# Ten loads for the next phase: one request of 5 MB, or ten pieces of 512 KB behind the tiles' stores

## Chip, cores and metric

The kernel runs on one core of a Trainium2 chip. A core has five engines with a program each: TensorE (PE: matmuls), VectorE (DVE), ScalarE (ACT), GpSimd (POOL) and SyncE (SP), which here only asks for DMA transfers. The transfers of all engines are carried out by 16 DMA engines. The metric is the time of one execution on the device in microseconds (us), lower is better.

## What is computed

A network of two layers on 4 x 512 tokens of 512 features, each with a mixer and a feed-forward part, a residual and a layer norm behind each. Only the start of the first mixer, a Mamba2 block, matters here:

```python
xz = x @ in_proj_w.T                       # 512 -> 2 x 1024 features
x_branch, z_branch = jnp.split(xz, 2, axis=-1)
y = conv(x_branch, conv_w)                 # causal, 4 taps, per feature
x_branch = silu(y + conv_b)
proj = x_branch @ x_proj_w.T               # 1024 -> X (1024), dt (16), B (128), C (128)
# ... chunked scan with X, dt, B, C ...
Y = Y * silu(z_branch)
return Y @ out_proj_w.T
```

The product `x_proj_w` and all that follows are the next phase. Every product is taken in three matmuls of rounded high and low parts (`product`, L82): hi*hi, hi*lo, lo*hi.

## The kernel before

**The input projection** (`mixer`, L129) handles the tokens in four batches of 512 (`NB` = 4, `SEQ` = 512), and in each batch eight tiles of 128 features (`IT` = 8): 32 tiles, numbered n = 8 b + j from 0 to 31. For each tile PE makes two products, one for the x branch and one for the z branch, of 12 matmuls each (`batch` of PE, L828), into four PSUM banks `acc` in turn: the x product of tile n uses the bank of tile n - 2, and so does the z product. Behind PE the tile passes through this chain (`batch` of ACT, L628, and of DVE, L1065): ACT scales the product with the last tap (L633), DVE adds three taps (L1071), ACT takes the silu (L639) and writes the rounded high part `out_hi` (L642), ACT writes the silu of z, `out_z` (L645), DVE writes the low part `out_lo` (L1062). `out_hi`, `out_lo` and `out_z` have two buffers each, used by even and odd tiles.

**The stores.** SP sends each tile's three results to DRAM, 256 KB each, in the order of its program: `xh` (L349), `zs` (L351), and `xl` of the tile before (L344). ACT may write `out_hi` of tile n only when the store `xh` of tile n - 2 has landed:

```python
act.wait_ge(s_sh[j % 2], turn)                       # L640
```

and PE may start the z product of tile n only when ACT has read z of tile n - 2:

```python
pe.wait_ge(s_zo, n - 1 + 2)                          # L835, s_zo starts at 2
```

Its x product waits in the same way for the taps of tile n - 2 (L837). So a late store holds ACT, and through ACT's queue PE.

**The loads for the next phase.** When the first batch is stored, the buffer `pre` that held the tokens is free, and SP asks for what the next phase reads first: five small tensors (L366 to L369), six of the eight row blocks of `x_wx` (3 MB, L371; `STAGED` = 6), `x_wbc` (1 MB, L372), and the first 128 tokens of `xh` and `xl`, read back from DRAM (512 KB each, L377 and L378, behind a wait for the first batch's stores). All count on one semaphore, `s_early`. Its first readers are in the last batch: ACT at tile 24 (`ahead`, L563) and PE after the first product of tile 24 (L797).

The batches 1 and 2 are a hardware loop on SP, ACT, PE and DVE. Everything is ordered by hand, engine by engine. Nothing plans or reorders.

Of the kernel before, what the change touches and what calls it, by code (L numbers as in the profile page):

```python
# [12 lines left out]
P = 128  # L13
# [5 lines left out]
DI = 2 * DM  # L19
# [109 lines left out]
def mixer(nc, t, ident):  # L129
# [3 lines left out]
    with ExitStack() as ctx:  # L133
# [175 lines left out]
        @block.sync  # L309
        def _(sp):  # L310
            def x_load(c, slot):
                for i, n in enumerate(("xh", "xl")):
                    sp.dma_start(raw(xin[slot][:, i]),
                                 t[n][:, :, bass.ds(c * P, P)].rearrange("j p n -> p j n")).then_inc(s_lx[slot], 16)

            def z_load(c):
                sp.dma_start(z_raw[:], t["zs"][:, :, bass.ds(c * P, P)].rearrange("j p n -> p j n")).then_inc(s_lz, 16)

            def load_x(b):
                sp.dma_start(x_tok[:, b], t["x"][b].rearrange("(c p) d -> p c d", p=P)).then_inc(s_x[b], 16)  # L320

            def load_w(g):
                if g >= 2:
                    sp.wait_ge(s_wlo, g - 1)
                sp.dma_start(w_raw[:, g % 2], t["in_w"][:, g]).then_inc(s_w[g % 2], 16)

            for c in range(CPB):
                sp.dma_start(x_tok[:, 0, c], t["x"][0, c * P:(c + 1) * P, :]).then_inc(s_x0[c], 16)
            load_w(0)
            sp.dma_start(cw[:], t["conv_w"]).then_inc(s_small, 16)  # L330
            sp.dma_start(cb[:], t["conv_b"]).then_inc(s_small, 16)
            load_w(1)
            for b in range(1, NB):
                load_x(b)
                if b + 1 < GRP:
                    load_w(b + 1)
            for i in range(2):
                sp.sem_inc(s_sh[i], 16)
                sp.sem_inc(s_sl[i], 16)
                sp.sem_inc(s_sz[i], 16)  # L340

            def store_lo(b, j):
                sp.wait_ge(s_xl, b * IT + j + 1 + 2)
                sp.dma_start(t["xl"][j][:, bass.ts(b, SEQ)], raw(out_lo[:, j % 2])).then_inc(s_sl[j % 2], 16)  # L344

            def batch(b, last=False):
                for j in range(IT):
                    sp.wait_ge(s_xo, b * IT + j + 1 + 2)
                    sp.dma_start(t["xh"][j][:, bass.ts(b, SEQ)], raw(out_hi[:, j % 2])).then_inc(s_sh[j % 2], 16)  # L349
                    sp.wait_ge(s_zo, b * IT + j + 1 + 2)  # L350
                    sp.dma_start(t["zs"][j][:, bass.ts(b, SEQ)], out_z[:, j % 2]).then_inc(s_sz[j % 2], 16)  # L351
                    if j:
                        store_lo(b, j - 1)
                    if last and j == 3:
                        sp.wait_ge(s_zacc, LASTB * IT + TPG // 2)
                        sp.dma_start(stage(6), t["x_wx"][:, 6]).then_inc(s_wl[0], 16)
                    if last and j == 5:
                        sp.wait_ge(s_zacc, LASTB * IT + TPG)
                        sp.dma_start(stage(7), t["x_wx"][:, 7]).then_inc(s_wl[1], 16)
                        for i in range(2):  # L360
                            sp.wait_ge(s_sz[i], 16 * (IT // 2 + 1))
                        z_load(0)
                store_lo(b, IT - 1)

            batch(0)
            sp.dma_start(wdt[0:NH, 0:DI], t["x_wdt"]).then_inc(s_early, 16)  # L366
            sp.dma_start(wdt[0:NH, DI:DI + NH], t["dtw"]).then_inc(s_early, 16)
            for n, name in enumerate(("dtb", "a_log", "d_skip")):
                sp.dma_start(per_head[:, n], t[name]).then_inc(s_early, 16)  # L369
            sp.wait_ge(s_xT, NB * KT)  # L370
            sp.dma_start(pre[:, 0:STAGED * DI], t["x_wx"][:, 0:STAGED].rearrange("p k n -> p (k n)")).then_inc(s_early, 16)  # L371
            sp.dma_start(pre[:, STAGED * DI:STAGED * DI + IT * 2 * NS],  # L372
                         t["x_wbc"].rearrange("p k n -> p (k n)")).then_inc(s_early, 16)
            for i in range(2):
                sp.wait_ge(s_sh[i], 16 * (IT // 2 + 1))
                sp.wait_ge(s_sl[i], 16 * (IT // 2 + 1))
            sp.dma_start(raw(x0[:, 0]), t["xh"][:, :, 0:P].rearrange("j p n -> p j n")).then_inc(s_early, 16)  # L377
            sp.dma_start(raw(x0[:, 1]), t["xl"][:, :, 0:P].rearrange("j p n -> p j n")).then_inc(s_early, 16)  # L378
            with sp.Fori(1, LASTB) as b:
                batch(b)  # L380
            batch(LASTB, True)
            sp.wait_ge(s_zacc, ROWS)
            x_load(1, 1)
            for i in range(WO):
                sp.dma_start(wo_part(wo_raw, i), t["out_w"][:, i]).then_inc(s_ol[i], 16)
            for i in range(2):
                sp.wait_ge(s_sh[i], 16 * (ROWS // 2 + 1))
                sp.wait_ge(s_sl[i], 16 * (ROWS // 2 + 1))
                sp.wait_ge(s_sz[i], 16 * (ROWS // 2 + 1))

            def step(g, slot, turn, first, left):
                if left == 2:
                    sp.wait_ge(s_p0, g + 1)
                    sp.wait_ge(s_p1, g + 1)
                    x_load(g + 2, 1 - slot)
                if not first:
                    sp.wait_ge(s_x1, g)
                    sp.dma_start(t["x1"][bass.ds(g * P - P, P), :], rr[:]).then_inc(s_out, 16)
                    sp.wait_ge(s_out, 16 * g)
                sp.dma_start(rr[:], t["x_rows"][bass.ds(g * P, P), :]).then_inc(s_lr, 16)  # L400
                if left:
                    sp.wait_ge(s_g, g + 1)
                    z_load(g + 1)
            chunks(sp, step)
            sp.wait_ge(s_x1, NCH)
            sp.dma_start(t["x1"][TOK - P:TOK, :], rr[:]).then_inc(s_out, 16)
            sp.wait_ge(s_out, 16 * NCH)
# [79 lines left out]
        def _(act):  # L487
# [72 lines left out]
            def ahead(j):  # L560

                if j == 0:
                    act.wait_ge(s_early, 144)  # L563
                    act.wait_ge(s_wlo, GRP)
                    nc.scalar.activation(wb_hi[:, :, NH:BC], stage_bc, ACT.Copy).then_inc(s_bwhi, 1)
                if j == 1:
                    act.wait_ge(s_zacc, LASTB * IT)
                    x_weights(0)
                if j == 2:
                    act.wait_ge(s_wdt, 1)  # L570
                    nc.scalar.activation(wb_hi[:, :, 0:NH], WDT.rearrange("p (k n) -> p k n", k=IT),
                                         ACT.Copy).then_inc(s_bwhi, 1)
                    x_weights(1)
                if j == 3:
                    x_weights(2)
                if j == 4:
                    bc_copy(0)
                    b_high(0, True)
                    x_weights(3)
                if j == 5:  # L580
                    nc.scalar.activation(a_pos, a_pos, ACT.Exp).then_inc(s_apos, 1)
                    dt_exp(0)
                    turned_copy(0)
                    c_high(0)
                if j == 6:
                    x_weights(4)
                    act.wait_ge(s_zacc, LASTB * IT + TPG // 2)
                    x_weights(5)
                if j == 7:
                    act.wait_ge(s_sum, 1)  # L590
                    nc.scalar.activation(c_hi[:], CT, ACT.Copy).then_inc(s_ch, 1)
                    x_weights(6)
# [84 lines left out]
        def _(pe):  # L677
# [116 lines left out]
            def ahead(m):  # L794

                if m == 0:
                    pe.wait_ge(s_early, 144)  # L797
                    for kt in range(IT):
                        ins = pe.matmul(WDT[:, kt * NH:(kt + 1) * NH], wdt[0:NH, bass.ts(kt, P)], dtw,
                                        start=True, stop=True)  # L800
                    ins.then_inc(s_wdt, 1)
                if m == 7:
                    pe.wait_ge(s_bwlo, 2)
                    bc_proj(0)
                if m == 9:
                    turn_bc(0, True)
                if m == 11:
                    cb_product(0, True)
                if m == 14:
                    pe.wait_ge(s_tri, 2)  # L810
                    pe.wait_ge(s_const, 6)
                    a_sums(0, True)
# [2056 lines left out]
```

## Time and profile before

| | |
|---|---|
| median of 3 runs | 2368.57 us (2367.68 to 2369.22) |
| profiled execution | 2367.82 us, of which the profile's span is 2366.1 us |
| PE busy | 2271.9 us, 96% of the span |
| DVE, ACT, POOL busy | 1577.5, 888.7, 762.1 us |
| mean granted TensorE clock | 0.987 of full speed (2.4 GHz) |
| DMA | 155.41 MB, mean 66 GB/s |

The times are device times. The profile is of one execution with its own time, 0.75 us under the median. PE is busy nearly throughout, so the time follows PE: what counts is where PE stands idle or runs at the lower clock, and what held it there. In the windows view each line is a stretch of the span and its length, then the busy time and the count of instructions of PE, of PE's weight loads (PEld), of DVE, ACT and POOL, the granted clock, the mean busy share of the DMA engines (it can read slightly over 1 in short stretches) and GB/s. In the timeline each line is an instruction with its start, its duration and, in brackets, the idle time of its engine before it and who ended it. SPq rows are SP's DMA requests: the duration there is the time of the request, not of the transfer. The start-to-start distance of the matmuls is what they cost. Their durations overlap.

### The profile page before, as it was taken

What the parts mean: (1) busy time and instruction counts of PE and PEld (TensorE: products, weight loads), DVE (VectorE), ACT (ScalarE), POOL (GpSimd) and SP (SyncE); (2) the same over time, 40 slices, a digit from 0 to 9 for tenths busy, and PEclk for the clock granted to TensorE, in tenths of its full rate; (3) what the DMA queues carried; (4) which work ended last, traced back from release to release, by engine and by line L of the source; (5) the groups of instructions that cost most, each with busy time, mean ns of one, the idle gap of its engine ahead of it and who ended that gap; (6) DMA issues with size and microseconds to landing.
All of it is one profiled execution on the core that took longest, in us unless ns stands there. A gap on an engine that the chain in (4) does not pass through costs nothing.

```text
span 2366.1 us, 30896 instructions
## 1 busy us (share of the span) xinstructions
PE 2271.9 (96%) x10746; PEld 1864.7 (79%) x10746; DVE 1577.5 (67%) x2392; ACT 888.7 (38%) x1441; POOL 762.1 (32%) x571
## 2 busy tenths in 40 slices
PE   8899999999969999999999899999999899999997
PEld 7787788888857888888887688777778778888885
DVE  5557777777747856674455666576677887766665
ACT  5456333333324322332232444234344434444441
POOL 0002544444412222251111533234233533333331
PEclk9999999999979999999999999999999999999999
DMA  5746222222132001000000111221111021111110
GB/s 205 224 146 188 63 71 71 71 75 74 56 111 107 36 1 36 23 1 19 1 1 27 57 52 55 106 81 54 54 54 54 27 89 54 53 53 53 53 36 36
DMA packets 91015, 155.41 MB, mean 66 GB/s; under 512 B 6288, under 2 KB 55440, under 8 KB 84256
## 3 DMA queue, kind: packets, MB, share of 16 engines
q1 hardware_dynamic: 90912, 154.07, 19.3%
q8 instruction: 61, 1.00, 0.2%
q14 instruction: 42, 0.34, 0.0%
HBM read 114.20 MB, written 39.85 MB: 65 GB/s over the span
## 4 chain that ended last, share of the span: by engine, by line
PE 61%; DVE 6%; issue 2%; ACT 1%; POOL 1%; DMA 0%; SPq 0%; POOLq 0%; DVEq 0%; ACTq 0%
PE attn_pvk L1120 4%; PE attn_pvk L1121 4%; PE attn_pvk L1122 4%; PE attn_pq L1120 2%; PE attn_pq L1121 2%; PE attn_pq L1122 2%; PE attn_po L1120 2%; PE attn_po L1121 2%; PE attn_po L1122 2%; PE attn_pv L1120 2%; PE attn_pv L1121 2%; PE attn_pv L1122 2%; PE attn_pv L85 2%; PE attn_pv L87 2%; PE attn_pv L86 2%
## 5 line engine op out<-in xcount | busy, mean ns | idle before, releaser
L2491 DVE TENSOR_TENSOR moe_a_lo<-moe_up_raw,moe_a_hi 128x512 fp32r<-128x512 f32 x192 | 183.0, 969 | 154.8 <-ACT moe_a_hi L1954 154.7
L1836 POOL TENSOR_TENSOR moe_h_lo<-moe_c_t,moe_h_hi 128x512 fp32r<-128x512 f32 x96 | 128.4, 1337 | 356.3 <-ACT moe_h_hi L1954 356.2
L1120 PE MATMUL attn_pvk<-moe_b_hi,moe_a_hi 128*128 128x512 f32 x512 | 200.9, 392 | 14.0 <-ACT moe_c_last L2080 6.0
L1122 PE MATMUL attn_pvk<-moe_b_hi,moe_a_lo 128*128 128x512 f32 x512 | 199.8, 390 | 0.0
L1121 PE MATMUL attn_pvk<-moe_b_lo,moe_a_hi 128*128 128x512 f32 x512 | 199.8, 390 | 0.0
L1954 ACT ACTIVATE moe_c_t<-attn_pvk 128x512 f32<-128x512 f32 x192 | 113.2, 596 | 186.5 <-PE attn_pvk L1122 184.5
L1231 POOL TENSOR_TENSOR ffn_h_lo<-ffn_h_f,ffn_h_hi 128x512 fp32r<-128x512 f32 x64 | 89.8, 1402 | 266.6 <-ACT ffn_h_hi L1284 266.6
L2006 ACT ACTIVATE moe_c_t<-moe_c_t 128x512 f32<-128x512 f32 x96 | 60.4, 629 | 241.1 <-DVE moe_c_t L2563 241.1
L1427 DVE SCALAR_TENSOR_TENSOR acc<-attn_pvk,ffn_wts,acc 128x512 f32<-128x512 f32 x128 | 91.2, 749 | 88.8 <-PE attn_pvk L87 88.5
L1954 ACT ACTIVATE moe_a_hi<-moe_up_raw 128x512 fp32r<-128x512 f32 x192 | 116.0, 624 | 56.4 <-POOL moe_up_raw L1806 56.4
L1120 PEld LDWEIGHTS attn_pvk<-moe_b_hi,moe_a_hi 128*128 128x128 f32 x512 | 96.4, 188 | 38.0 <-issue 11.3
L2523 DVE SCALAR_TENSOR_TENSOR acc<-attn_pv,moe_wts,acc 128x512 f32<-128x512 f32 x123 | 91.8, 747 | 41.4 <-PE attn_pv L1122 40.4
L1071 DVE SCALAR_TENSOR_TENSOR mix_conv<-mix_acc,mix_cw,mix_conv 128x511 f32<-128x511 f32 (+2 forms) x96 | 71.9, 748 | 69.3 <-ACT mix_conv L633 67.0
L2563 DVE TENSOR_TENSOR moe_c_t<-moe_c_t,attn_po 128x512 f32<-128x512 f32 x128 | 86.4, 684 | 43.2 <-ACT moe_c_t L1954 37.9
L2523 DVE SCALAR_TENSOR_TENSOR acc<-attn_pq,moe_wts,acc 128x512 f32<-128x512 f32 x133 | 99.2, 746 | 22.3 <-PE attn_pq L1122 19.3
L85 PE MATMUL mix_acc<-mix_x_hi,mix_w_hi 128*128 128x512 f32 (+1 forms) x256 | 102.2, 399 | 11.6 <-issue 5.7
L1806 POOL TENSOR_TENSOR moe_up_raw<-moe_up_raw 128x512 f32<-128x512 f32 x32 | 52.0, 1624 | 188.9 <-DVE moe_a_lo L2491 188.8
L1122 PEld LDWEIGHTS attn_pvk<-moe_b_hi,moe_a_lo 128*128 128x128 f32 x512 | 96.4, 188 | 20.3
L1121 PEld LDWEIGHTS attn_pvk<-moe_b_lo,moe_a_hi 128*128 128x128 f32 x512 | 96.4, 188 | 19.5
L1120 PE MATMUL attn_pq<-moe_dn_hi,moe_h_hi 128*128 128x512 f32 x266 | 106.1, 399 | 2.7 <-DVE acc L2523 2.7
L85 PE MATMUL mix_tp<-mix_wx_hi,mix_x 128*128 128x512 f32 x256 | 106.4, 416 | 0.0
L1121 PE MATMUL attn_pq<-moe_dn_lo,moe_h_hi 128*128 128x512 f32 x266 | 104.2, 392 | 0.0
(487 smaller groups left out, 6573.2 us busy)
## 6 DMA issues: line engine op xcount, KB each, us to landing
moe_up_raw<-in_e_up SPq DMA_DIRECT2D x28, 1024.0 KB, 5.7
moe_dn_raw<-in_e_dn SPq DMA_DIRECT2D x28, 512.0 KB, 3.6
xh<-mix_out_hi SPq DMA_DIRECT2D x32, 256.0 KB, 2.6
zs<-mix_out_z SPq DMA_DIRECT2D x32, 256.0 KB, 3.2
xl<-mix_out_lo SPq DMA_DIRECT2D x32, 256.0 KB, 3.4
mix_x<-xh SPq DMA_DIRECT2D x16, 512.0 KB, 4.1
mix_x<-xl SPq DMA_DIRECT2D x16, 512.0 KB, 5.3
mix_z_raw<-zs SPq DMA_DIRECT2D x16, 512.0 KB, 3.9
```

The lines of the kernel that those rows point to most:

```text
L85: pe.matmul(out, lh, rh, start=first, stop=False)
L1071: nc.vector.scalar_tensor_tensor(out=conv[:, j % 2, d:SEQ], in0=acc[:, 2 * j % 4, 0:SEQ - d], scalar=cw[:, j, TAPS - 1 - d:TAPS - d], in1= ...
L1120: pe.matmul(out, lh, rh, start=first, stop=False, skip_group_check=True)
L1121: pe.matmul(out, lh, rl, start=False, stop=False, skip_group_check=True)
L1122: return pe.matmul(out, ll, rh, start=False, stop=True, skip_group_check=True)
L1231: nc.gpsimd.tensor_tensor(h_lo[:, f], h_f[:, f % 2], raw(h_hi[:, f]), ALU.subtract).then_inc(s_hlo, 1)
L1427: stt(out=acc[:, ch], in0=pd[c], scalar=wts[:, ch, bass.ds(F * u + f, 1)], in1=acc[:, ch], op0=ALU.mult, op1=ALU.add).then_inc(s_acc, 1)
L1836: tt(h_lo[:, m, tok], src, raw(h_hi[:, m, tok]), ALU.subtract).then_inc(s_hlo, 1)
L1954: copy = lambda out, src: nc.scalar.activation(out, src, ACT.Copy)
L2491: tt_(a_lo[q][:], src, raw(a_hi[q][:]), ALU.subtract).then_inc(s_alo, 1)
L2523: stt(out=acc[:, ch], in0=bank, scalar=wts[:, ch, w] if isinstance(w, slice) else wts[:, ch, bass.ds(w, 1)], in1=acc[:, ch], op0=ALU.mult, ...
L2563: tt_(c_t[tile][:, i], c_t[tile][:, i], bank(i), ALU.add).then_inc(sem, 1)
```

## The change

SP no longer asks for the 5 MB in one go before batch 1. A new function `ahead(i)` holds ten requests of 512 KB: six row blocks of `x_wx`, two halves of `x_wbc`, and the two read-backs of `xh` and `xl`. One of them stands behind the stores of each tile of batch 1 (i = 0 to 7) and of the first two tiles of batch 2 (i = 8, 9). The wait for the first batch's stores moves to i = 8. The five small loads stay where they were. SP's hardware loop over batches 1 and 2 becomes a Python loop, so its rows are written out. The two waits on `s_early` ask for 15 transfers (16 * 15 = 240) instead of 9 (144).

```diff
+            def ahead(i):
+                if i < STAGED:
+                    sp.dma_start(stage(i), t["x_wx"][:, i]).then_inc(s_early, 16)
+                elif i < STAGED + 2:
+                    k0 = (i - STAGED) * IT // 2
+                    sp.dma_start(stage_bc[:, k0:k0 + IT // 2], t["x_wbc"][:, k0:k0 + IT // 2]).then_inc(s_early, 16)
+                elif i < STAGED + 4:
+                    if i == STAGED + 2:
+                        for n in range(2):
+                            sp.wait_ge(s_sh[n], 16 * (IT // 2 + 1))
+                            sp.wait_ge(s_sl[n], 16 * (IT // 2 + 1))
+                    part = i - STAGED - 2
+                    sp.dma_start(raw(x0[:, part]),
+                                 t[("xh", "xl")[part]][:, :, 0:P].rearrange("j p n -> p j n")).then_inc(s_early, 16)
...
                     if j:
                         store_lo(b, j - 1)
+                    if 0 < b < LASTB:
+                        ahead((b - 1) * IT + j)
...
             sp.wait_ge(s_xT, NB * KT)
-            sp.dma_start(pre[:, 0:STAGED * DI], t["x_wx"][:, 0:STAGED].rearrange("p k n -> p (k n)")).then_inc(s_early, 16)
-            sp.dma_start(pre[:, STAGED * DI:STAGED * DI + IT * 2 * NS],
-                         t["x_wbc"].rearrange("p k n -> p (k n)")).then_inc(s_early, 16)
-            for i in range(2):
-                sp.wait_ge(s_sh[i], 16 * (IT // 2 + 1))
-                sp.wait_ge(s_sl[i], 16 * (IT // 2 + 1))
-            sp.dma_start(raw(x0[:, 0]), t["xh"][:, :, 0:P].rearrange("j p n -> p j n")).then_inc(s_early, 16)
-            sp.dma_start(raw(x0[:, 1]), t["xl"][:, :, 0:P].rearrange("j p n -> p j n")).then_inc(s_early, 16)
-            with sp.Fori(1, LASTB) as b:
+            for b in range(1, LASTB):
                 batch(b)
...
-                    act.wait_ge(s_early, 144)
+                    act.wait_ge(s_early, 16 * (5 + STAGED + 4))
...
-                    pe.wait_ge(s_early, 144)
+                    pe.wait_ge(s_early, 16 * (5 + STAGED + 4))
```

On SP, at the step from batch 0 to batch 1, this stands before, from the last small load on (the `DMA pre` rows are the weights, the `mix_x` rows the read-backs, the rows behind the branch the first tile of batch 1):

```order
L369 DMA mix_heads<-in_d_skip 128x16
L371 DMA pre<-in_x_wx 128x6144 [waits mix_x_transposed]
L372 DMA pre<-in_x_wbc 128x2048
L377 DMA mix_x_50<-xh 128x8x128 [waits mix_x_hi_stored1,mix_x_lo_stored1,mix_x_lo_stored0,mix_x_hi_stored0]
L378 DMA mix_x_50<-xl 128x8x128
L379 UNCONDITIONAL_BRANCH
L379 ISA
L349 ISA [waits mix_x_hi_out]
L349 DMA xh<-mix_out_hi 128x512
L351 DMA zs<-mix_out_z 128x512 [waits mix_z_tile_out]
```

And now, at the same place (L364, L366 and L344 are the stores of xh, zs and xl, L348 is the first branch of `ahead`):

```order
L386 DMA mix_heads<-in_d_skip 128x16
L364 DMA xh<-mix_out_hi 128x512 [waits mix_x_hi_out,mix_x_transposed]
L366 DMA zs<-mix_out_z 128x512 [waits mix_z_tile_out]
L348 DMA pre<-in_x_wx 128x1024
L364 DMA xh<-mix_out_hi 128x512 [waits mix_x_hi_out]
L366 DMA zs<-mix_out_z 128x512 [waits mix_z_tile_out]
L344 DMA xl<-mix_out_lo 128x512 [waits mix_x_lo_out]
L348 DMA pre<-in_x_wx 128x1024
```

Four requests of 5 MB together stood ahead of the first store of batch 1, and none does now. Each tile's stores have one 128x1024 request behind them.

At the end of batch 1 and the start of batch 2, on SP too, this stands now (L351 is the second half of `x_wbc`, L358 the read-backs). The lone L344 row closes batch 1:

```order
L351 DMA pre<-in_x_wbc 128x1024
L344 DMA xl<-mix_out_lo 128x512 [waits mix_x_lo_out]
L364 DMA xh<-mix_out_hi 128x512 [waits mix_x_hi_out]
L366 DMA zs<-mix_out_z 128x512 [waits mix_z_tile_out]
L358 DMA mix_x_50<-xh 128x8x128 [waits mix_x_hi_stored1,mix_x_lo_stored1,mix_x_lo_stored0,mix_x_hi_stored0]
L364 DMA xh<-mix_out_hi 128x512 [waits mix_x_hi_out]
L366 DMA zs<-mix_out_z 128x512 [waits mix_z_tile_out]
L344 DMA xl<-mix_out_lo 128x512 [waits mix_x_lo_out]
L358 DMA mix_x_50<-xl 128x8x128
```

The read-backs moved from ahead of batch 1 to tiles 16 and 17. The instructions of PE, DVE, ACT and POOL, their order and the semaphores they wait on are the same in both kernels.

## Rows read from the trace of the kernel before

**Rows 1.** PE's waits in 60 to 216 us: total, times, longest.

```profile
PE mix_acc L85 <- ACT mix_out_z L645: 5.2, 1, 5.2
PE mix_tp L710 <- DVE mix_cb_m L930: 2.0, 1, 2.0
```

**Rows 2.** Windows: stretch, us, PE, PEld, DVE, ACT, POOL, clock, DMA, GB/s.

```profile
76.00:100.00 24.00, 18.77 (x76) 15.05 (x75) 8.53 (x12) 8.05 (x14) 0.00 (x0) 0.86 0.90 308
92.00:94.00 2.00, 0.00 (x0) 0.00 (x0) 0.00 (x0) 0.47 (x1) 0.00 (x0) 0.50 1.07 305
100.00:162.00 62.00, 62.00 (x275) 51.12 (x273) 34.23 (x48) 29.37 (x48) 1.53 (x8) 1.00 0.51 153
```

**Rows 3.** Timeline of ACT around the stall and where it catches up with PE.

```profile
80.33 0.63 ACT L642 ACTIVATE mix_out_hi<-mix_conv 128x512 fp32r<-128x512 f32 x1
84.60 0.63 ACT L639 ACTIVATE mix_conv<-mix_conv 128x512 f32<-128x512 f32 x1 [2.48 <-DVE mix_conv L1071]
93.53 0.63 ACT L642 ACTIVATE mix_out_hi<-mix_conv 128x512 fp32r<-128x512 f32 x1 [8.30 <-DMA xh<-mix_out_hi]
...
98.66 0.63 ACT L642 ACTIVATE mix_out_hi<-mix_conv 128x512 fp32r<-128x512 f32 x1
103.65 0.63 ACT L642 ACTIVATE mix_out_hi<-mix_conv 128x512 fp32r<-128x512 f32 x1
104.19 0.58 ACT L645 ACTIVATE mix_out_z<-mix_acc 128x512 f32<-128x512 f32 x1
...
134.99 0.78 ACT L633 ACTIVATE mix_conv<-mix_acc,mix_cb,mix_cw 128x512 f32<-128x512 f32 x1 [0.27 <-PE mix_acc L87]
```

**Rows 4.** Timeline of SP's requests around the stall.

```profile
75.05 0.43 SPq L369 DMA_DIRECT2D mix_heads<-in_d_skip  x1
...
77.02 6.44 SPq L378 DMA_DIRECT2D mix_x<-xl  x1
83.82 5.22 SPq L349 DMA_DIRECT2D xh<-mix_out_hi  x1
```

**Rows 5.** Timeline of PE before and behind the stall.

```profile
75.85 0.39 PE L85 MATMUL mix_acc<-mix_x_hi,mix_w_hi 128*128 x1
...
89.22 0.39 PE L87 MATMUL mix_acc<-mix_x_hi,mix_w_lo 128*128 x1
94.84 0.80 PE L85 MATMUL mix_acc<-mix_x_hi,mix_w_hi 128*128 x1 [5.23 <-ACT mix_out_z L645]
...
98.69 0.40 PE L85 MATMUL mix_acc<-mix_x_hi,mix_w_hi 128*128 x1
```

**Rows 6.** DMA requests by line: number, size, median us to landing.

```profile
xh<-mix_out_hi SPq DMA_DIRECT2D x32, 256.0 KB, 2.6
mix_x<-xl SPq DMA_DIRECT2D x16, 512.0 KB, 5.3
pre<-in_x_wx SPq DMA_DIRECT2D x1, 3072.0 KB, 11.4
mix_wx_raw<-in_x_wx SPq DMA_DIRECT2D x2, 512.0 KB, 4.7
```

**Rows 7.** SP's first and last request of tile 27, a 512 KB load.

```profile
185.16 0.33 SPq L349 DMA_DIRECT2D xh<-mix_out_hi  x1
...
186.96 0.46 SPq L356 DMA_DIRECT2D mix_wx_raw<-in_x_wx  x1
```

**Rows 8.** Windows of 1 us in and behind tile 27, and at 203 us.

```profile
188.00:189.00 1.00, 1.00 (x6) 0.84 (x5) 0.00 (x0) 0.00 (x0) 0.00 (x0) 1.00 1.18 207
191.00:192.00 1.00, 1.00 (x7) 0.83 (x6) 0.96 (x2) 0.45 (x1) 0.04 (x1) 1.00 0.00 0
203.00:204.00 1.00, 1.00 (x6) 0.83 (x5) 0.96 (x3) 0.55 (x1) 0.00 (x0) 1.00 1.13 129
```

**Rows 9.** The first reader of the early loads, on ACT.

```profile
162.87 1.90 ACT L565 ACTIVATE mix_wb_hi<-pre 128x2048 fp32r<-128x2048 f32 x1
```

**Rows 10.** A window of 4 us in the next part, with PE busy throughout.

```profile
716.00:720.00 4.00, 4.00 (x12) 3.15 (x11) 2.13 (x5) 1.69 (x2) 0.00 (x0) 0.57 0.96 360
```

## Prediction

> **What bounds the kernel now.** The page says 96% PE, so I read only what keeps PE from working in the stretch that the change touches, 60 to 216 us. PE's waits come first [rows 1]: two of note, 5.2 us for `out_z` of ACT and 2.0 us for a DVE mask near the end of the phase. The windows [rows 2] place the first: between 76 and 100 us PE is busy for 18.77 of 24 us at a mean clock of 0.86, while the DMA engines are busy to 0.90 at 308 GB/s. From 100 to 162 us PE has no gap at all, at full clock, with the DMA engines half idle (0.51). The timeline of ACT gives the cause [rows 3]: `out_hi` of tile 10 is ready to be written at 84.60 + 0.63 = 85.2, but starts at 93.53, 8.30 us late, when the store `xh` of tile 8 has landed. SP's rows say why that store was late [rows 4]. SP was free for it at 75.5, when the last small load (75.05 + 0.43) was asked for. It then asked for the four large loads, the last request took 6.44 us (the queue was full), and the store was asked for at 83.82, took 5.22 us to ask for, and queued behind the 5 MB. The 3 MB load alone takes 11.4 us to land, against 2.6 us for such a store in the median [rows 6].
>
> So this is one stall with one cause: three results of a tile cannot leave because 5 MB that nobody reads until 162.87 [rows 9] stands ahead of them.
>
> **The change part by part.** *The stall.* PE's matmuls follow each other every (89.22 - 75.85) / 59 = 0.2266 us ahead of the stall (59 steps between those two rows of the pattern), so the next one was due at 89.22 + 0.23 = 89.45, and it starts at 94.84 [rows 5]: 5.39 us. *The clock.* Behind the gap the granted clock is 0.50, which is 1.2 GHz [rows 2]. The nine steps from 94.84 to 98.69 take 3.85 us instead of 9 x 0.2266 = 2.04 [rows 5]: 1.81 us. Together 7.20 us of PE's time are lost here.
>
> *What is late next when it goes.* PE, at 89.45, needs ACT to have finished z of tile 10. ACT and DVE go round a tile in 103.65 - 98.66 = 4.99 us when nothing holds them, PE in 24 x 0.2266 = 5.44 us. Without the stall `out_hi` of tile 10 starts at 80.33 + 4.99 = 85.3 and z of it ends about 1.1 us later (z starts 0.54 after `out_hi` and takes 0.58 [rows 3]), at 86.4: 3.0 us ahead of PE. The distance grows by 0.45 us per tile until ACT waits for PE, as it does in the trace from 134.99 on. So nothing on ACT or DVE takes the stall's place, and at tile 24, where the last batch begins, all engines stand to each other as they do now. What follows (the 2.0 us for the mask, the wait at the start of the next part) hangs on PE, ACT and on SP's requests made after them, and moves with them. I give it zero.
>
> *The added requests.* SP gets one more request per tile on ten tiles. Such a request is 0.46 us, behind 1.8 us for the three stores (185.16 to 186.96) [rows 7]. That is 2.3 us of a tile's 5, so it is hidden. A tile now moves 3 x 256 + 512 KB = 1.31 MB. At the 308 GB/s of the crowded stretch that is 4.3 us of a tile's 4.99 to 5.44, so the DMA engines keep up. The trace also has one tile that already looks like the new ones, tile 27, with `x_wx` block 6 behind its stores: from its first request at 185.16 [rows 7] to a silent queue by 191 at the latest [rows 8], under 5.84 us, the requests' 1.8 us included. If I take all of that as transport, every tile hands 0.4 us to the next, 4 us over ten tiles. The room is larger: a store `xh` is asked for some 0.8 us after `out_hi` starts (its 0.63 us and a little), its buffer is wanted 2 x 4.99 us after that start, and it lands in 2.6 us, which leaves 9.98 - 0.8 - 2.6 = 6.6 us. So the added wait is bounded by 0 on both readings. I take 0, and keep the slow readings for the rivals. A gain from smaller stores' queues, below nothing, has no place: PE has no other gap to give back in 100 to 162 us.
>
> *The late loads.* The last piece, the read-back of `xl`, goes out with the stores of tile 17, seven tiles of 5.44 us ahead of those of tile 24, so at about 121 us, and lands in 5.3 us [rows 6]. Its readers come at 162.87 - 7.2 = 155.7: about 29 us of cover. The moved wait, for the stores of batch 0, was passed by 77.02 before [rows 4] and now stands some 38 us later, so it is met. The written-out loop costs SP nothing that PE sees.
>
> The trace bears on a rule here. The 512 KB pieces land in 4.7 us in the median and the 3 MB in 11.4 [rows 6], so six pieces one after another would take 28 us. The Trainium skill ("DMA: Bandwidth & Descriptors", section Bandwidth and its Rules for kernel authors) says to batch transfers to at least 1 MiB, and its fit of a fixed 2.0 us plus bytes over 436 GB/s makes a tile's four transfers an estimated 11.0 us if they went one by one. By the rule the change would hurt: 11.0 us per tile against 5.44 is far past the room above. The trace disagrees for this queue: tile 27's four transfers were over in 5.84 us, so their fixed parts overlap.
>
> *Sum.* -5.39 - 1.81 + 0 = -7.20 us. The profiled execution goes from 2367.82 (span 2366.1 and 1.7 around it) to 2360.6. It is 0.75 under the median of the runs shown, so the median goes from 2368.57 to 2361.4.
>
> **The rivals.** Let t be the time in which the DMA engines move a tile's 1.31 MB. The lag over ten tiles is 10 (t - 5.44), and what exceeds the room of 6.6 us becomes a wait of ACT and of PE.
>
> *Part of the stall comes back.* The slowest 1 us of tile 27 moved 207 GB/s [rows 8]. If all ten tiles went at that, t = 6.33, the lag 8.9 and the wait 2.3 us. With that alone 2363.7, and with a lower clock behind it (1.8 us) 2365.5. I put this case at 2364.6. Against it: 207 was one microsecond with the requests just changing from stores to a load, and the mean of the crowded stretch is 308.
>
> *The pieces choke the stores, slower than before.* From t = 6.82 us on (192 GB/s) the wait exceeds the 7.20 us won. At 168 GB/s, the mean of the two slowest microseconds here (207 and 129 [rows 8], the second with a read-back in 512-byte rows like i = 8 and 9), t = 7.8, the wait 17.0 and the time 2368.6 + 9.8 = 2378.4. For it: in the new kernel eight tiles in a row have a load, not one. Against it: all the rows of longer stretches. The skill's rule above, if it held, would be this case too.
>
> *It does not do what it says.* The first store of batch 1 might be late for another reason than the 5 MB, for instance the small loads ahead of it, or the stall might move to another buffer (`out_lo` or `out_z`, with the same two turns). Then nothing changes: 2368.6. Against it: SP is free at 75.5, before the store's data, and the other stores queue in the same place.
>
> **How the numbers follow.** The forecast case has a chance of 0.86, the partial one 0.07, no change 0.04, slower 0.03. A median of three tells 0.2% (4.7 us) from no change, so faster means under 2363.8. The forecast case's own spread is the clock's: the granted clock also falls in stretches where PE is busy (0.57 in 4 us [rows 10], worth 4 x 0.43 = 1.7 us), and the shift may win or lose one such dip, so 2359.7 to 2363.1. The partial case reaches to 2365.5. I take 2359.6 to 2364.5, which leaves out most of the last two cases, part of the partial one and the tails. Faster: 0.86. The partial and the empty case give 0.11 for no change, and slower has 0.03.
>
> **What would show it.** Right: no PE gap over 1 us between 65 and 160 us, clock 1.00 throughout there. The `xh` store of tile 8 asked for near 76.0 and landed before 85.3. No wait of ACT L651 (now the write of `out_hi`) for a DMA. ACT waits for PE from about tile 13 on instead of 19. ACT's copy of `x_wbc` at about 155.7. The wait for the mask still 2.0 us. DMA share in the tiles of batch 1 near 0.8. Wrong: a DMA wait on `out_hi` or `out_lo` in later tiles with landings over 9 us (pieces choke), a gap at 89 of the old size (other cause), or the 7 us gained by 155 us and gone again by the start of the next part.

## Result: 0.29% faster, and the profile after

| | before | after |
|---|---|---|
| median | 2368.94 us (20 runs, 2367.68 to 2375.01) | 2363.11 us (20 runs, 2359.78 to 2367.76) |
| profiled execution | 2367.82 us, span 2366.1 | 2363.05 us, span 2361.3 |

The ratio is 0.9971 with a 95% interval of 0.9965 to 0.9978: 6.9 us (5.2 to 8.3) less. The difference of the two medians is 5.8 us. The forecast was 2361.4 us, 7.2 us less, in a range of 2359.6 to 2364.5.

PE's waits in 60 to 212 us of the new kernel, the view of [rows 1]:

```profile
PE mix_tp L719 <- DVE mix_cb_m L939: 2.0, 1, 2.0
PE mix_acc L85 <- DVE mix_conv L1080: 0.7, 1, 0.7
```

The wait of 5.2 us for `out_z` is gone, and the one for the mask is still 2.0 us. The 0.7 us stand at 66.6 us, ahead of the change. The kernel before has the same wait there, so it is no part of what follows. The windows that answer to [rows 2], the second 7 us shorter here (stretch, length, busy PE, PEld, DVE, ACT, POOL, clock, DMA share, GB/s):

```profile
76.00:100.00 24.00, 24.00 (x108) 19.87 (x107) 12.70 (x19) 12.10 (x20) 0.00 (x0) 1.00 0.86 245
100.00:155.00 55.00, 55.00 (x245) 45.53 (x244) 30.31 (x43) 25.53 (x41) 0.95 (x6) 1.00 0.76 206
```

PE is busy for all 24 us where it had 18.77, at full clock. The transfers are spread: 245 GB/s instead of 308 in the first stretch, 206 instead of 153 in the second. SP's requests in tiles 8 to 10, against [rows 4]:

```profile
76.86 0.43 SPq L386 DMA_DIRECT2D mix_heads<-in_d_skip  x1
77.86 0.34 SPq L364 DMA_DIRECT2D xh<-mix_out_hi  x1
78.29 0.39 SPq L366 DMA_DIRECT2D zs<-mix_out_z  x1
78.72 0.46 SPq L348 DMA_DIRECT2D pre<-in_x_wx  x1
82.79 0.33 SPq L364 DMA_DIRECT2D xh<-mix_out_hi  x1
83.28 1.37 SPq L366 DMA_DIRECT2D zs<-mix_out_z  x1
84.70 0.43 SPq L344 DMA_DIRECT2D xl<-mix_out_lo  x1
85.17 0.44 SPq L348 DMA_DIRECT2D pre<-in_x_wx  x1
```

The store `xh` of tile 8 is asked for as soon as its data is there, and none of these requests takes over 1.4 us. ACT's `out_hi` of tiles 9 and 10, against 80.33 and 93.53 in [rows 3]:

```profile
82.14 0.63 ACT L651 ACTIVATE mix_out_hi<-mix_conv 128x512 fp32r<-128x512 f32 x1
87.13 0.63 ACT L651 ACTIVATE mix_out_hi<-mix_conv 128x512 fp32r<-128x512 f32 x1
```

4.99 us apart, the free pace, instead of 13.20. But tile 9 stands at 82.14, 1.8 us later than before: something ahead of the change took time. And behind it the clock falls where it did not before (windows again):

```profile
158.00:160.00 2.00, 2.00 (x11) 1.68 (x11) 1.93 (x4) 1.42 (x2) 0.00 (x0) 0.88 1.03 286
160.00:162.00 2.00, 2.00 (x6) 1.60 (x5) 0.96 (x7) 1.16 (x2) 0.00 (x0) 0.50 0.05 16
162.00:164.00 2.00, 2.00 (x8) 1.56 (x8) 0.00 (x0) 0.60 (x1) 0.00 (x0) 0.77 0.35 131
```

Set side by side by the same instructions of ACT, the two profiles are apart by +1.8 us at tile 9, -5.5 at tile 23, -3.8 at tile 31 and -4.8 at the end. So two questions are left: is the start chance, and is the fall at 158 to 164 us the price of the change?

### The profile page after: what moved, and what is told of

Same layout as the page of the kernel before. It is cut to its first block, busy times and chain, and to the rows that moved or that the text cites. A ratio compares the mean times of both kernels' runs of the same rounds, so it can differ in the third digit from the quotient of the medians.

```text
span 2361.3 us, 30818 instructions
## 1 busy us (share of the span) xinstructions
PE 2271.6 (96%) x10746; PEld 1865.4 (79%) x10746; DVE 1576.9 (67%) x2392; ACT 888.9 (38%) x1441; POOL 761.7 (32%) x571
## 4 chain that ended last, share of the span: by engine, by line
PE 61%; DVE 6%; issue 2%; ACT 1%; POOL 1%; DMA 0%; POOLq 0%; SPq 0%; DVEq 0%; ACTq 0%
PE attn_pvk L1129 4%; PE attn_pvk L1131 4%; PE attn_pvk L1130 4%; PE attn_pq L1129 2%; PE attn_pq L1130 2%; PE attn_pq L1131 2%; PE attn_po L1129 2%; PE attn_po L1131 2%; PE attn_po L1130 2%; PE attn_pv L1129 2%; PE attn_pv L1130 2%; PE attn_pv L1131 2%; PE attn_pv L85 2%; PE attn_pv L87 2%; PE attn_pv L86 2%
## 5 line engine op out<-in xcount | busy, mean ns | idle before, releaser
L1129 PE MATMUL attn_po<-moe_b_hi,moe_a_hi 128*128 128x512 f32 x256 | 100.8, 394 | 4.4 <-DVE moe_c_t L2572 4.4
```

Source lines behind the costliest of these rows:

```text
L1129: pe.matmul(out, lh, rh, start=first, stop=False, skip_group_check=True)
```

## Experiments

All profiles are compared by four starts on ACT, read from their timelines. "Stretch" is `out_hi` of tile 9 to `out_hi` of tile 23, which holds the ten requests and the stall that they remove. "Last batch" is tile 23 to tile 31. The medians scatter from one series of runs to the next (the kernel before: 2368.94 to 2370.60), so the last column gives the kernel before in the same series. In us:

| profile | first conv | stretch | last batch | median of runs | before in the same series |
|---|---|---|---|---|---|
| before | 18.03 | 80.41 | 50.37 | 2368.94 | 2368.94 |
| before, again | 18.90 | 80.72 | 50.38 | 2368.93 | 2370.39 |
| before, third | 20.07 | 81.00 | 52.00 | 2370.34 | 2370.60 |
| loop written out | 18.94 | 80.58 | 50.37 | 2371.48 | 2370.39 |
| 5 MB behind tile 8 | 18.42 | 77.74 | 50.36 | 2366.22 | 2368.96 |
| 3 MB behind tile 8 | 20.12 | 73.13 | 52.01 | 2363.34 | 2368.96 |
| ten pieces | 19.83 | 73.14 | 51.98 | 2363.11 | 2368.94 |
| ten pieces, again | 17.96 | 73.14 | 50.37 | 2364.22 | 2368.96 |
| ten pieces, third | 19.30 | 73.14 | 52.00 | 2363.48 | 2370.60 |
| pieces, dt products spread | 18.61 | 73.15 | 52.54 | 2364.08 | 2368.96 |
| twice the loads | 18.33 | 73.12 | 50.99 | 2363.87 | 2370.39 |
| three times the loads | 19.14 | 79.43 | 50.15 | 2367.86 | 2370.39 |

**The new kernel twice more** (no edit).

> The changed kernel once more, as the measure for the others and for a second profile. My theory: the change gives 7.2 us on PE between 80 and 155 us in every execution, and what is measured beyond or below that is the start of the kernel and the clock. In the profile of the first execution the first conv of ACT (L642, tile 0) came 1.8 us later than in the kernel before, since the first weights landed late, and the clock fell for about 4 us behind the 16 small matmuls at 156.6 to 158.5. If both are chance of one execution, one or both are absent here (tile 0 back at 18.0, clock 1.00 from 156 to 164), while the distance from tile 9 to tile 23 on ACT stays at 73.4 us (160.74 - 80.33 - 7.2 = 73.2 by the prediction). Rival: the clock falls there in every execution of the new kernel, because the change brings it about; then 5.5 us is what the change is worth, not 7.2.

> The kernel with the pieces a third time. By now the distance from out_hi of tile 9 to that of tile 23 is 73.14 us in both of its profiles and 80.41 to 80.72 in three with the 5 MB ahead of tile 8: expected 73.1 again. What moves the whole by 1 to 2 us from one execution to the next lies outside: ACT's first conv (17.96 to 20.12 so far, in all kernels), and a fall of the clock in the last batch, which makes its 50.37 us 52.0. Theory: these are chance, so this time may lie anywhere from 2360 to 2367. Rival: the fall in the last batch comes with the change (4 of 5 profiles of kernels without the early gap had one, none of 4 with a gap near 95 us): then it is here again more likely than not.

Ratios to before 0.9980 (0.9971 to 0.9988) and 0.9969 (0.9959 to 0.9980), which is 4.7 and 7.3 us less. The stretch is 73.14 us in all three profiles. The first conv is at 17.96 and 19.30, and the last batch is free of a fall in one and has it in the other. The profile of `pieces_again` in the window that had the fall:

```profile
158.00:160.00 2.00, 2.00 (x11) 1.65 (x10) 1.10 (x7) 1.57 (x3) 0.00 (x0) 1.00 0.09 31
160.00:162.00 2.00, 2.00 (x11) 1.65 (x10) 0.00 (x0) 0.29 (x1) 0.00 (x0) 1.00 0.71 262
```

**The kernel before twice more** (no edit).

> The kernel before once more, for a second profile. My theory: the 5 MB stand ahead of tile 8's store in every execution, so the stall is here again, out_hi of tile 10 waiting 8 us for the store and PE 5 us, with the lower clock behind it; the distance on ACT from out_hi of tile 9 to that of tile 23 is 80.4 us again (160.74 - 80.33), against 73.0 in both profiles of the kernel with the pieces. The start (ACT's first conv at 18.0) and falls of the clock in the light stretches of PE at 162 and 208 may differ, as they did between profiles of the new kernel. Rival: the stall was an accident of the one profile, or differs much from execution to execution; then the distance is off by more than 1 us.

> The kernel before a third time, for the same count: distance 80.4 to 80.7 by my theory, with the gap of 5.2 us and the lower clock behind it. If the last batch shows a fall of the clock here (52.0 instead of 50.37 us), the change does not bring it about. If not, that stays open.

The stall is in both, with PE's waits of 5.2 and 5.0 us for `out_z`, and stretches of 80.72 and 81.00. The third profile has a fall of the clock in the last batch:

```profile
166.00:168.00 2.00, 2.00 (x13) 1.83 (x13) 1.89 (x3) 1.81 (x2) 0.00 (x0) 0.86 1.08 307
168.00:170.00 2.00, 2.00 (x6) 1.52 (x6) 1.47 (x8) 1.26 (x2) 0.00 (x0) 0.50 0.33 102
```

So the change is not needed for that fall, and the rival in its strong form, that only the change brings it about, is out. The weaker form stays open: that the fall comes more often now. It stands in two of the three profiles of the pieces and in one of three of before. Over all kernels below that keep the group of small matmuls as it was, and leaving out the one with three times the loads, it stands in three of five profiles without the early gap (pieces, 3 MB, twice the loads) and in one of five with it. So few profiles can't tell that from chance. If it is so, the change pays a part of 1.6 us for it.

**Only SP's loop written out.**

```diff
-            with sp.Fori(1, LASTB) as b:
+            for b in range(1, LASTB):
                 batch(b)
```

> The kernel before with only SP's hardware loop over batches 1 and 2 written out, the 5 MB as before. My theory: SP's loop costs PE nothing, so the stall and the time are those of the kernel before: the same within 1 us, the distance from tile 9 to tile 23 at 80.4 us. Rival: the loop's own rows (a branch, register steps and a wait per store) held the first store of batch 1 back; then the distance and the time fall by a part of the 7.4 us.

2371.48 us against 2370.39 for the kernel before in the same series, ratio 1.0002 (0.9991 to 1.0014), stretch 80.58, the stall as before:

```profile
ACT mix_out_hi L642 <- DMA xh<-mix_out_hi: 8.3, 1, 8.3
PE mix_acc L85 <- ACT mix_out_z L645: 5.4, 1, 5.4
```

The loop costs nothing that PE sees. So the gain comes from the loads, which were both moved and cut. The two kernels with large loads below tell which of the two it was.

**5 MB at once, behind two stores of tile 8.**

```diff
+                if i == 0:
+                    sp.dma_start(pre[:, 0:STAGED * DI],
+                                 t["x_wx"][:, 0:STAGED].rearrange("p k n -> p (k n)")).then_inc(s_early, 16)
+                if i == 0:
+                    sp.dma_start(pre[:, STAGED * DI:STAGED * DI + IT * 2 * NS],
+                                 t["x_wbc"].rearrange("p k n -> p (k n)")).then_inc(s_early, 16)
+                if i == 0:
...
+                    sp.dma_start(raw(x0[:, 0]), t["xh"][:, :, 0:P].rearrange("j p n -> p j n")).then_inc(s_early, 16)
+                if i == 0:
+                    sp.dma_start(raw(x0[:, 1]), t["xl"][:, :, 0:P].rearrange("j p n -> p j n")).then_inc(s_early, 16)
```

> The same four large requests as before, 5 MB at once, but behind the first two stores of tile 8 instead of ahead of them. My theory (queueing): the next store, xh of tile 9, is asked for when SP has got rid of the requests, near 85, and lands some 16 us after the large requests, near 95. out_hi of tile 11 is due at 90.3, so ACT waits about 5 us, DVE about as long for xl of tile 8. PE leads by 3.5 us by then, so its gap is 1 to 2 us without or with a short fall of the clock: time 1 to 3 us over the kernel with the pieces. Rival A (only the size of a request counts): a stall of 5 us with its clock as before, the time of the kernel before. Rival B (only the first store had to get ahead): no wait at all, the time of the pieces.

2366.22 us against 2364.22 for the pieces in the same series: 2.0 us slower by the medians, which is inside the expected 1 to 3. By the stretch, which repeats far better, it is 4.6 us, so the parts were larger than expected. ACT's and PE's waits and SP's requests:

```profile
DVE mix_out_lo L1071 <- DMA xl<-mix_out_lo: 8.1, 1, 8.1
ACT mix_out_hi L651 <- DMA xh<-mix_out_hi: 6.2, 1, 6.2
PE mix_acc L85 <- ACT mix_out_z L654: 2.7, 1, 2.7
```

```profile
78.43 0.38 SPq L357 DMA_DIRECT2D mix_x<-xh  x1
78.85 10.75 SPq L359 DMA_DIRECT2D mix_x<-xl  x1
89.64 3.04 SPq L364 DMA_DIRECT2D xh<-mix_out_hi  x1
```

I had SP free near 85. The last request held it for 10.75 us, so the next store was asked for at 89.64. Behind PE's gap of 2.7 us the clock fell at 98 to 104 us, which I had allowed only as a short one. Both rivals are out: one store ahead of the 5 MB takes off part of the stall, not all and not nothing.

**3 MB, 1 MB and the two read-backs, apart.** The same four branches with `i == 2` for `x_wbc` and `i == 8` and `i == 9` for the read-backs.

> Four large requests, but apart: 3 MB behind tile 8's stores, 1 MB behind tile 10's, the two read-backs behind tiles 16 and 17. My theory: 3 MB take 9.6 us at 328 GB/s, the store xh of tile 9 is asked for 5 us later and lands within 5.4 + 2.6 = 8 us of that, its buffer is wanted 9.2 us after the asking: no wait on PE, and the same time as with the ten pieces within 0.5 us. Rival (the pieces must be small: SP or the stores choke behind any large one): a wait of ACT on a DMA and a PE gap over 1 us, 2 us or more slower than the pieces.

2363.34 us against 2364.22 for the pieces in the same series, the stretch 73.13. ACT waits 0.8 us and DVE 4.0 us for stores:

```profile
DVE mix_out_lo L1071 <- DMA xl<-mix_out_lo: 4.0, 2, 3.0
ACT mix_out_hi L651 <- DMA xh<-mix_out_hi: 0.8, 1, 0.8
```

PE sees nothing of it. But 3 MB is near the edge: I had the store `xh` of tile 9 landing within 8 us, and the slowest `xh` took 10.0 us, more than the 9.2 that its buffer had. ACT's wait of 0.8 us stayed hidden behind its lead over PE. So up to 3 MB the size of a piece costs PE nothing here, and the gain came from the place of the loads. What counts is that what stands ahead of a store is gone within the time that its buffer has.

**Two and three times the loads in tiles 12 to 21.**

```diff
                     if 0 < b < LASTB:
                         ahead((b - 1) * IT + j)
+                        more((b - 1) * IT + j)
...
+            def more(i):
+                for _ in range(2 - (1 if i < STAGED + 4 else 0) if 4 <= i < 14 else 0):
...
+                    sp.wait_ge(s_blk[k], 16 * loaded[k])
...
+                    sp.dma_start(stage(k), t["x_wx"][:, k]).then_inc(s_blk[k], 16)
```

(3 instead of 2 in the second kernel. Each block has a semaphore of its own, `s_blk`, on which ACT waits before its first read. SP waits on it too before it loads a block again, which held SP for 3.9 us in all in the second kernel.)

> The changed kernel, with 1 MB of loads behind each of the tiles 12 to 21 instead of 512 KB or none: blocks of x_wx are loaded again into the place where they stand already (14 loads more, 7.3 MB). With its stores a tile then moves 1.84 MB. By my model (308 GB/s, a tile of 5.44 us, room 6.6 us) t = 5.96, the lag over ten tiles 5.2 us: no wait of PE, and the time of the pieces within 1 us. By the slow reading (207 GB/s) t = 8.9, lag 34 us, PE waits 28 us. By the rule of a fixed 2 us for each transfer, one after another, it would be still more. So this shows how much room the ten pieces left.

> As the double one, with 1.5 MB of loads behind each of the tiles 12 to 21 (24 loads more than in the kernel with the pieces). A tile moves 2.36 MB, which takes 7.66 us at 308 GB/s, 7.2 at the 328 GB/s that the 5 MB reached, against a tile of 5.44. By my model the lag over ten tiles is 18 to 22 us, less the room of 6.6 us and some 5 us by which PE leads: PE waits 6 to 11 us in tiles 15 to 21, and with a lower clock between the waits the kernel is 8 to 15 us slower than with the pieces. Rival (the engines take far more than 308 GB/s from a queue that is never empty, the 516 GB/s seen for 2 us): no wait, the time of the pieces.

With twice the loads: 2363.87, stretch 73.12, no gap of PE beyond the 0.7 us at 66 us that every kernel here has. With three times: 2367.86, stretch 79.43. PE's gaps and the waits for stores in the latter, then the DMA of both (first the twofold, then the threefold kernel) from 120 to 150 us:

```profile
DVE mix_out_lo L1085 <- DMA xl<-mix_out_lo: 21.5, 8, 5.9
PE mix_acc L85 <- DVE mix_conv L1094: 4.2, 4, 2.7
ACT mix_out_hi L665 <- DMA xh<-mix_out_hi: 2.0, 2, 1.5
```

```profile
120.00:150.00 30.00, 30.00 (x134) 24.84 (x133) 16.50 (x24) 14.30 (x24) 0.00 (x0) 1.00 1.03 354
```

```profile
120.00:150.00 30.00, 29.75 (x131) 24.10 (x130) 14.24 (x20) 13.70 (x22) 0.00 (x0) 1.00 1.05 356
```

The choke of the slow rival exists, but between 1.84 and 2.36 MB per tile, not at 1.31. I expected 6 to 11 us of waits in PE. Of the 4.2 us, 0.7 are the wait at 66 us, so the loads cost 3.5. I expected 8 to 15 us in the time. From tile 9 to tile 31 it was 6.1 us more than in the profile of the pieces without a fall (129.58 against 123.51), and by the ratios to the kernel before (0.9992 against 0.9969 to 0.9980) 3 to 5 us. The model had 308 GB/s. The engines moved 356 from 120 to 150 us, so a tile took 2.36 / 0.356 = 6.6 us and not 7.66. The low part's store was the first to be late, for 21.5 us in all, and it led to the largest gap of PE, behind which the clock fell to 0.50 at 172 us:

```profile
167.47 0.69 DVE L1085 TENSOR_TENSOR mix_out_lo<-mix_conv,mix_out_hi 128x512 fp32r<-128x512 f32 x1 [4.98 <-DMA xl<-mix_out_lo]
170.45 0.50 PE L85 MATMUL mix_acc<-mix_x_hi,mix_w_hi 128*128 128x512 f32 x1 [2.71 <-DVE mix_conv L1094]
```

That gap lies behind tile 23. Inside the stretch PE lost only 0.8 us. The rest of the 6.3 us by which the stretch grew is the lead that ACT lost.

**The dt products spread.** The eight small products are of two matmuls each as PE runs them. Each pair now stands behind three large matmuls of the next two products (each such product has four groups of three), and not between blocks of 12 as the expectation puts it. The loop over them in PE's `ahead`, not shown, goes.

```diff
                                       kt == 0, kt == KT - 1)
+                        if last and m in (1, 2):
+                            dt_weights((m - 1) * KT + kt)
```

> The changed kernel with one more edit: PE's eight small products for the dt weights (16 matmuls in 1.95 us behind the first product of tile 24) are spread singly between the blocks of 12 large matmuls of the next two products. The same work in the same total time. Theory: the clock falls for about 4 us behind the dense group of small ones in many executions (cost 1.7 us each time), and does not where they stand singly: faster than the pieces by 1 to 1.7 us in the median and with less spread. Rival: the fall had another cause (chance, or the DMA): no difference within 0.5 us, and profiles with the fall at the same place.

2364.08 us, no better than 2364.22 for the pieces in the same series. In its profile the clock holds at the old place and falls at 204 to 208 us instead, near the wait for the mask:

```profile
158.00:160.00 2.00, 2.00 (x10) 1.20 (x8) 1.77 (x8) 1.32 (x4) 0.00 (x0) 1.00 0.42 139
206.00:208.00 2.00, 2.00 (x7) 1.52 (x6) 1.89 (x5) 1.17 (x3) 0.00 (x0) 0.50 0.02 7
```

The clock did hold behind the spread matmuls, but "the same work in the same total time" was wrong. PE's rows show what the spreading costs, first here, then with the dense group (`pieces_again`):

```profile
157.01 0.40 PE L87 MATMUL mix_acc<-mix_x_hi,mix_w_lo 128*128 128x512 f32 x1
157.34 0.39 PE L806 MATMUL mix_tp<-mix_wdt 16*128 16x16 f32 x2
...
158.23 0.39 PE L87 MATMUL mix_acc<-mix_x_hi,mix_w_lo 128*128 128x512 f32 x1
```

```profile
154.44 0.39 PE L87 MATMUL mix_acc<-mix_x_hi,mix_w_lo 128*128 128x512 f32 x1
154.76 1.95 PE L808 MATMUL mix_tp<-mix_wdt 16*128 16x16 f32 x16
...
157.22 0.39 PE L87 MATMUL mix_acc<-mix_x_hi,mix_w_lo 128*128 128x512 f32 x1
```

Three large matmuls alone take 3 x 0.2266 = 0.68 us. With a pair of small ones among them they take 1.22, so a pair costs 0.53 us and eight pairs 4.3. The dense group costs 2.78 - 0.68 = 2.1. The spread form is thus about 2.2 us longer at full clock, and its last batch is 52.54 us, 2.17 over the 50.37 of a batch without a fall. That is more than the 1.6 us which a fall costs. No version was faster than the pieces beyond the scatter.

**The group of small matmuls three times over**, in both kernels.

```diff
-                    for kt in range(IT):
+                    for kt in [*range(IT)] * 3:
```

> The kernel with the pieces, with the group of 16 small matmuls in the last batch done three times over (the same values again), 5.8 instead of 1.95 us of light work on PE with no gap. Theory: a busy PE still loses its clock behind light work, which is what cost 1.65 us behind this group in two of the profiles. With three times the length the fall comes surely: clock 0.50 within or behind the group, last batch 50.4 + 3.9 + 1.6 to 3 us. Rival (the fall has to do with something else, the DMA or chance): clock 1.00 throughout and a last batch of 54.3 us.

> The same threefold group in the kernel before. Theory: light work costs the clock here as well, so the last batch is as long as in the pieces kernel with the group three times, within 1.7 us, and the early gap with its own fall makes no difference to it. Rival (a fall at 95 us spares a later one): clock 1.00 behind the group here, and 54.3 us for the last batch, while the pieces kernel has a fall.

One profile each. The last batch is 55.53 us with the pieces and 55.50 before. The group takes 5.69 and 5.67 us instead of 1.95, so that is 50.37 + 3.7 for the added work + 1.4. The clock falls behind the group in both, first the pieces, then before:

```profile
160.00:162.00 2.00, 2.00 (x11) 1.87 (x11) 0.00 (x0) 0.08 (x1) 0.00 (x0) 0.67 0.35 131
162.00:164.00 2.00, 2.00 (x6) 1.52 (x6) 0.00 (x0) 0.00 (x0) 0.00 (x0) 0.50 0.00 0
```

```profile
168.00:170.00 2.00, 2.00 (x12) 1.86 (x12) 0.00 (x0) 0.17 (x1) 0.00 (x0) 0.70 0.35 131
170.00:172.00 2.00, 2.00 (x6) 1.52 (x6) 0.00 (x0) 0.00 (x0) 0.00 (x0) 0.50 0.00 0
```

Here too a fall at 95 us does not spare a later one. Two profiles with a fall of two support the theory of the light work. They do not prove it, since the plain group has one in four of eleven.

## Why the prediction was right

*The stall and its cause: right.* 5 MB ahead of the first store of batch 1, and nothing else: moving only the requests removes it, and writing out only the loop does not.

*The size: right in the stretch.* The two terms, 5.39 us of gap and 1.81 us of lower clock, make 7.20. The stretch shrank from 80.41, 80.72 and 81.00 us in three profiles of before to 73.14 in three of after, by 7.3 to 7.9 us. The gap varied by 0.2 us only (5.0 to 5.2). What varied more was the clock behind it.

*Nothing takes its place: right.* PE has no gap between 67 us and the mask in any profile of the pieces. The 2.0 us for the mask stayed.

*The added requests cost nothing: right, with more room than the bounds said.* The slowest landing of an `xh` store was 5.3 us after its request (9.7 before), where 9.2 were allowed. 1.84 MB per tile still cost nothing, so the partial case and the choke were too far off for the 0.10 that I gave them: I took the rates from windows of 1 us in which the kind of transfer changes (207 and 129 GB/s), and these say nothing of a lasting rate. But I worked out the room for `xh` alone. The store of the low part `xl` is asked for a tile later, lands after up to 7.9 us, and is the one that was waited for: DVE stood 1.4, 2.6 and 1.7 us for it in the three profiles of the pieces. This stayed hidden behind the lead of ACT and DVE over PE, which the bound on the room had left out.

The rule of at least 1 MiB per transfer (the Trainium skill, "DMA: Bandwidth & Descriptors", Bandwidth and Rules for kernel authors) did not bind: 3 MB in one request and in six gave a stretch of 73.13 and 73.14 us. The fixed 2.0 us per transfer are from another section of that page of the Trainium skill, "Anatomy of one DMA — SWDGE (gpsimd) path", a fit for transfers that GpSimd asks for, while here SP asks. They overlap here: with twice the loads a tile's five transfers passed at 354 GB/s, which is 1.84 / 0.354 = 5.2 us a tile.

*ACT waits for PE from tile 13 on: wrong, it is tile 17.* I had the gain per tile (0.45 us) but not the distance to make up. PE had no use of it.

*DMA share near 0.8 in batch 1: wrong*, 0.96 from 85 to 120 us at 269 GB/s.

*The median, 2361.4 against 2363.11:* 1.7 us off, inside the range. The span of the profiled run fell by 4.8 where the stretch fell by 7.3. The rest is the 1.8 us at the start and the fall at 158 to 164 us (1.6), less 1.0 won further on. The runs show these differences in both kernels: first conv at 18.03 to 20.07 before and 17.96 to 19.83 after, last batch 50.4 or 52.0, and from tile 31 to the end of the span 2153.6 to 2158.6 us before and 2154.0 to 2158.3 after. That last part is the largest, and what makes it was not looked into. I had given the clock 1.7 us either way and the rest nothing. So the mechanism and its 7.2 us are shown by the stretch. That the whole came out under 2363.8, my mark for faster, by 0.7 us is in part luck: the two later medians of the same kernel are 2363.48 and 2364.22, and the three series give 6.9, 4.7 and 7.3 us. The median before was itself 0.4 us higher over 20 runs than over three.

## What to carry to other kernels

A bulk load that nobody needs soon is not free just because the DMA engines are half idle: what counts is which transfers stand behind it in the same queue, and how long their buffers can wait. Work out that time for every store and not only the first (for `xh` here two tiles, 9.2 us from request to reuse, for `xl` less), keep the bytes ahead of any store under what it allows, and put the store first. Small pieces are then a matter of taste, large ones do as well. For a gain of 0.3%, compare the distance between two instructions on either side of the change over several profiles: it was 73.14 us three times with the pieces and repeated within 0.6 us before, where whole executions scattered over 8.

## What the runs showed of the hardware

- The DMA share does not tell the room left: 0.96 at 269 GB/s with the pieces, but 1.03 at 354 GB/s with twice the loads.
- Much unfinished work ahead holds the engine that asks: a 512 KB request took SP 6.44 us behind 4.5 MB [rows 4], and 10.75 us in the kernel with the 5 MB behind tile 8, where most take 0.33 to 0.5 us. That the queue was full then is the reading of these times, and no row shows it.
- A busy PE can lose its clock: behind 16 small matmuls (1.95 us, no gap) in four of eleven profiles, behind 48 of them in both that I tried, for 3 to 4 us each time and 1.4 to 1.6 us of time. That the light work is what does it is likely and not proven.
- Small matmuls are dearer singly than together: a pair among large ones cost PE 0.53 us, eight pairs in one group 2.1 us.
- The start varies: the first conv of ACT comes at 17.96 to 20.12 us with the same program ahead of it. What makes that was not looked into. Part of it goes with a clock of 0.50 at the first matmuls, which some profiles have, but the ones at 19.83, 20.07 and 20.12 do not.
